# A four-layer graph network on one core: one-hots of the targets compared by VectorE inside the loop, edge steps moved, the tail's products in float32r

## Time and profile before

| | us |
|---|---|
| median of 3 runs (lowest, highest) | 244.22 (243.98, 244.51) |
| the profiled execution | 244.86 |
| its span | 243.1 |
| TensorE busy | 230.7 |
| VectorE busy | 155.0 |
| ScalarE busy | 121.5 |
| GpSimd busy | 5.5 |

### The profile page before, as it was taken

One profiled execution on the slowest core, in us unless ns is written; L12 is line 12 of the kernel. 1 busy time (PEld: TensorE's weight loads), 2 busy tenths in 40 slices (PEclk: granted clock), 3 DMA queues, 4 the chain that ended last, 5 costly groups with the idle time before them and its releaser, 6 DMA issues.

```text
span 243.1 us, 3227 instructions
## 1 busy us (share of the span) xinstructions
PE 230.7 (95%) x1230; PEld 185.8 (76%) x1230; DVE 155.0 (64%) x274; ACT 121.5 (50%) x221; POOL 5.5 (2%) x17
## 2 busy tenths in 40 slices
PE   7999999997999999999999999999999999997980
PEld 4977888664766887888888888888888889996760
DVE  3948765687679655865856848758568455273625
ACT  0617289748639835745635646456356343244000
POOL 0000000001000000000000000000000000000001
PEclk9999999999999999999999999999999999999996
DMA  7999969920580000008041040140000000000001
GB/s 231 288 411 396 391 188 385 380 79 0 167 260 7 0 0 0 3 17 325 3 118 59 0 174 0 10 165 0 0 0 3 0 0 0 3 0 0 3 1 43
DMA packets 12039, 24.97 MB, mean 103 GB/s; under 512 B 988, under 2 KB 1908, under 8 KB 11640
## 3 DMA queue, kind: packets, MB, share of 16 engines
q1 hardware_dynamic: 11232, 24.25, 28.3%
q10 hardware_dynamic: 792, 0.51, 0.8%
HBM read 24.50 MB, written 0.26 MB: 102 GB/s over the span
## 4 chain that ended last, share of the span: by engine, by line
PE 89%; DVE 4%; ACT 2%; issue 2%; POOL 1%; POOLq 0%; DVEq 0%; ACTq 0%
PE bank L675 36%; PE bank L658 12%; PE bank L463 9%; PE bank L472 6%; PE bank L521 4%; PE bank L537 3%; PE bank L685 3%; PE bank L686 3%; PE bank L561 1%; PE bank L482 1%; PE bank L452 1%; ACT WsT L414 1%; PE bank L637 1%; PE bank L549 1%; PE bank L638 1%
## 5 line engine op out<-in xcount | busy, mean ns | idle before, releaser
L675 PE MATMUL bank<-W2hi,Hhi 128*128 128x512 f32 x128 | 49.8, 389 | 0.0
L675 PE MATMUL bank<-W2lo,Hhi 128*128 128x512 f32 x128 | 49.8, 389 | 0.0
L675 PE MATMUL bank<-W2hi,Clo 128*128 128x512 f32 x128 | 49.8, 389 | 0.0
L386 ACT ACTIVATE Mhi<-M 128x512 fp32r<-128x512 f32 x32 | 20.2, 632 | 45.4 <-DVE M L1011 45.4
L1016 DVE TENSOR_TENSOR Mlo<-M,Mhi 128x512 fp32r<-128x512 f32 x32 | 22.1, 689 | 24.4 <-ACT M L387 24.4
L1011 DVE TENSOR_TENSOR M<-bank,b2r 128x512 f32<-128x512 f32 x32 | 22.0, 687 | 12.7 <-PE bank L686 7.6
L675 PEld LDWEIGHTS bank<-W2hi,Hhi 128*128 128x128 f32 x128 | 24.0, 188 | 5.1
L675 PEld LDWEIGHTS bank<-W2lo,Hhi 128*128 128x128 f32 x128 | 24.0, 188 | 5.0
L675 PEld LDWEIGHTS bank<-W2hi,Clo 128*128 128x128 f32 x128 | 24.0, 188 | 5.0
L379 ACT ACTIVATE Hhi<-C 128x512 fp32r<-128x512 f32 x32 | 20.0, 624 | 12.4 <-DVE C L997 12.1
L297 ACT ACTIVATE C<-bank,cols 128x512 f32<-128x512 f32 x32 | 19.9, 685 | 10.5 <-PE bank L521 10.5
(11 more groups left out here) (201 smaller groups left out, 315.5 us busy)
## 6 DMA issues: line engine op xcount, KB each, us to landing
F<-in_L_gnn_W SPq DMA_DIRECT2D x2, 2048.0 KB, 14.6
W1raw<-in_L_gnn_W SPq DMA_DIRECT2D x1, 2048.0 KB, 23.7
ids<-in_src SPq DMA_DIRECT2D x2, 1024.0 KB, 13.1
W<-in_L_gnn_W SPq DMA_DIRECT2D x1, 2048.0 KB, 9.1
Wq<-in_L_gnn_Wq SPq DMA_DIRECT2D x4, 256.0 KB, 3.7
Wk<-in_L_gnn_Wk SPq DMA_DIRECT2D x4, 256.0 KB, 5.4
Wv<-in_L_gnn_Wv SPq DMA_DIRECT2D x1, 1024.0 KB, 9.6
ea<-in_edge_attr SPq DMA_DIRECT2D x1, 1024.0 KB, 11.6
```

Of the source, the lines that this page charges most:

```text
L386: act.activation(Mhi[:, t, :], M[:, t, :], ACT.Mish)
L675: done = mm(ST2[t][:, :], x[:, c, e], w[:, c, :], start=c == 0 and i == 0, stop=c == KC - 1 and i == 2)
```

## The change

1. The eight groups of turned target one-hots, their ScalarE copies and the ring of banks that they used are gone. `DT` is made by VectorE by comparing target ids that are broadcast to all partitions, as `ST` was.
2. Only groups 0 and 1 of `ST` and `DT` are made before the loop (two instructions each). The target ids for them go into the same buffers as the source ids, once these are read. For groups 2 to 7 the ids are loaded a second time and compared inside the loop, two groups ahead; `first_layer(g)` waits for them.
3. Edge steps 0 to 2 stand where the turns stood, step 3 in F1, 4 to 6 in F2.
4. The F2 load no longer waits for the turns; W2's load stands behind the target ids; the rows and weights of the later layers are loaded in the loop's sixth group.
5. The products of W4 and of layer 3 are made of three float32r terms each. The splits of W4, W_self, W_neigh and of their inputs are new instructions on ScalarE and VectorE.
6. The warm-up is six matmuls on a tile that VectorE fills first of all.
7. The softmax's sum over heads is by additions in place of `tensor_reduce`, and the copy `CTs` comes before `uniform`.

```diff
         def first_layer(g, js=range(KC), ks=range(len(terms))):
+                if g >= 2:
+                    pe.wait_ge(S["oh_ready"], 3 * (g - 1))
...
+            def loop_sources(g):
+                dve.wait_ge(S["loop_src_in"], 16)
+                v.tensor_scalar(ST_by_group[:, g], src_ids[:, g // 2, g % 2], iota_col[:, 0:1], None, ALU.is_equal).then_inc(S["oh_ready"], 1)
+            def loop_targets(g):
+                dve.wait_ge(S["loop_dst_in"], 32)
+                for h in range(2):
+                    v.tensor_scalar(DT_by_group[:, g, h], dst_ids[h][:, g // 2, g % 2], iota_col[:, 0:1], None,
+                                    ALU.is_equal).then_inc(S["oh_ready"], 1)
...
                 one_hot(g)
                 z2_out(g, 2)
+                if 1 <= g < G - 2:
+                    loop_sources(g + 2)
+                if g >= G - 2:
+                    weight_low(W4lo, W4, W4hi, (2 * (g - G + 2),), "w4")
                 message_low(g, 2)
                 z2_out(g, 3)
+                if g == 0:
+                    loop_sources(g + 2)
+                elif g < G - 2:
+                    loop_targets(g + 2)
+                if g >= G - 2:
+                    weight_low(W4lo, W4, W4hi, (2 * (g - G + 2) + 1,), "w4")
                 message_low(g, 3)
+                if g == 0:
+                    loop_targets(g + 2)
...
-            source_onehots(0)
+            for h in range(2):
+                first_onehots(ST_by_tile, "row_ids_in", h)
             dve.wait_ge(S["graphT_done"], 1)
...
-            source_onehots(1)
             dve.wait_ge(S["nx_ready"], 2)
             chain(v.tensor_tensor(xw[:, :], y[:, :], r("L0_gnn_b2"), ALU.add))
             xb = r("L0_gnn_be2")
             chain(v.tensor_tensor(xb, xs[:, :], xb, ALU.add))
+            for h in range(2):
+                first_onehots(DT_by_tile, "dst_ids_in", h)
             st = residual((bank[1], bank[2]), xw, S["f2_done"])
...
-            sp.wait_ge(S["pre_done"], C_UNIT)
             sp.wait_ge(S["ct_done"], 1)
             sp.dma_start(F2, w_view(a["L0_gnn_W2"])).then_inc(S["f2_in"], 16)
...
+            for h in range(2):
+                sp.wait_ge(S["st_ready"], h + 1)
+                sp.dma_start(other[f"ids{h}"], by_partition(a["dst"][E // 2 * h:E // 2 * (h + 1)], E // 2)).then_inc(S[f"dst_ids_in{h}"], 16)
             sp.dma_start(W2raw, w_view(a["L1_gnn_W2"])).then_inc(S["w2_in"], 16)
...
             sp.wait_ge(S["nx_ready"], 4)
+            for h in range(2):
+                sp.dma_start(loop_ids[f"dst_ids{h}"], by_partition(a["dst"][E // 2 * h:E // 2 * (h + 1)], E // 2)).then_inc(S["loop_dst_in"], 16)
+                if h == 0:
+                    sp.wait_ge(S["late_done"], 2 * KC)
+                    sp.dma_start(loop_ids["src_ids"], by_partition(a["src"], E)).then_inc(S["loop_src_in"], 16)
...
-            turn_onehots(Dbf, range(1, G))
-            pe.wait_ge(S["ea_lo"], 1)
+            pe.wait_ge(S["cols_ready"], 1)
+            pe.wait_ge(S["wc_lo"], 1)
+            edge_term(range(0, 1))
             turn_features(1)
+            edge_term(range(1, 3))
             transpose_halves(O_BANKS, y, S["nx_ready"], 0, S["nT_done"])
...
-            pe.wait_ge(S["ident_ready"], 1)
-            keep_warm(5, bank[2])
+            pe.wait_ge(S["warm_ready"], 1)
+            keep_warm(6, bank[2])
+            pe.wait_ge(S["ident_ready"], 1)
...
+            pe.wait_ge(S["u_hi"], 2)
+            for b in range(2):
+                columns_by(o_banks, uThi, W4hi, b, (0, 1), 0, None)
+                columns_by(o_banks, uThi, W4lo, b, (0, 1), None, None)
+            pe.wait_ge(S["u_lo"], 1)
+            for b in range(2):
+                columns_by(o_banks, uTlo, W4hi, b, (0, 1), None, None)
...
+            for h in range(2):
+                pe.wait_ge(S["xl_hi"], h + 1)
+                for b in range(2):
+                    columns_by(out_banks, xThi, WsThi, b, (2 * h, 2 * h + 1), None, None)
...
+            weight_low(WsTlo, WsT, WsThi, (1,), "ws")
+            st = bank_statistics((bank[5], bank[6]), S["g3_done"])
+            norms[0] += 1
+            v.bn_aggr(mv[:, :], st).then_inc(S["stat_ready"], 1)
+            weight_low(WsTlo, WsT, WsThi, (2,), "ws")
```

More of the change, by code:

```diff
@@ L77, in gnn_kernel @@
         ones2 = sb("ones2", [2, N], F32R)
+        warm = sb("warm", [P, P], BF16)
         uniform = sb("uniform", [P, N])
@@ L136, in gnn_kernel @@
         W3, W4, WsR, WnR = chunks(last["W3"], 2 * KC), chunks(last["W4"], KC), chunks(last["WsR"], KC), chunks(last["WnR"], KC)
-        WsT, WnT, uT, aggT, nmT = (chunks(last[n], KC) for n in ("WsT", "WnT", "uT", "aggT", "nmT"))
+        WsT, WnT, uT, aggT = (chunks(last[n], KC) for n in ("WsT", "WnT", "uT", "aggT"))
+        W4hi, WsThi, WnThi, xThi, xTlo, nmThi, nmTlo, uThi = (chunks((late if n == "WsThi" else last)[n], KC) for n in (
+            "W4hi", "WsThi", "WnThi", "xThi", "xTlo", "nmThi", "nmTlo", "uThi"))
+        W4lo, WsTlo, WnTlo, uTlo = (chunks(rest[n], KC) for n in ("W4lo", "WsTlo", "WnTlo", "uTlo"))
         G1, G2 = chunks(last["G1"], KC), last["G2"]
@@ L424, in _ @@
             act.activation(r1g, bank[3][:, 0:HID2], ACT.Relu).then_inc(S["g1_ready"], 1)
+            ws_high(2)
             act.wait_ge(S["g2_done"], 1)
             act.activation(p1g, bank[4][:, 0:N], ACT.Copy).then_inc(S["g2_ready"], 1)
+            ws_high(3)
+            act.wait_ge(S["wt_ready"], 2 * KC)
+            for c in range(KC):
+                act.activation(WnThi[:, c, :], WnT[:, c, :], ACT.Copy).then_inc(S["wn_hi"], 1)
+            for h in range(2):
+                act.wait_ge(S["nT_done"], 4 + h + 1)
+                act.activation(half(flat(xThi), h), (bank[1], bank[3])[h][:, 0:D // 2], ACT.Copy).then_inc(S["xl_hi"], 1)
+            act.wait_ge(S["nm_done"], 1)
+            act.activation(flat(nmThi), bank[2][:, :], ACT.Copy).then_inc(S["nm_hi"], 1)
             act.wait_ge(S["y_centred"], 1)
@@ L478, in keep_warm @@
             def keep_warm(n, b):
-                idle = ident[:, :].bitcast(BF16)
                 for _ in range(n):
[L482 to L497, removed]
+                    mm(b[:, :], warm[:, :], warm[:, :].unsqueeze(1).to_broadcast([P, 4, P]), start=True, stop=True)
             def turn_features(q):
@@ L813, in _ @@
             xT_flat = flat(xT[:, :, :])
+            v.memset(warm[:, :], 1.0).then_inc(S["warm_ready"], 1)
             chain(v.memset(stats[:, 2, :], 0.0))
@@ L916, in _ @@
                 dve.wait_ge(S["exp_done"], o + 1)
-                step = v.tensor_reduce(quarter(y, o), attn[:, o].rearrange("p j n -> p n j"), AX.X, ALU.add)
-            chain(step)
+                pairs, four = half(y, 1), quarter(y, o)
+                chain(v.tensor_tensor(pairs, attn[:, o, 0:2].rearrange("p j n -> p (j n)"), attn[:, o, 2:4].rearrange("p j n -> p (j n)"),
+                                      ALU.add))
+                chain(v.tensor_tensor(four, quarter(pairs, 0), quarter(pairs, 1), ALU.add))
             chain(v.tensor_tensor(total[:, :], quarter(y, 0), quarter(y, 1), ALU.add))
@@ L1066, in _ @@
             v.memset(ones, 1.0).then_inc(S["ones_ready"], 1)
+            for h in range(2):
+                dve.wait_ge(S["u_hi"], 2 * (h + 1))
+                dve.wait_ge(S["u_ready"], 2 * (h + 1))
+                v.tensor_tensor(half(flat(uTlo), h), half(flat(uT), h), half(flat(uThi), h).bitcast(F32), ALU.subtract).then_inc(S["u_lo"], 1)
             st = residual((bank[2], bank[4]), xw, S["o_done"])
```

184 lines of the change are left out of this document (115 added, 69 removed).

## The result

The changed kernel takes 247.73 us (247.31 to 248.07, 4 runs), the kernel before 244.10 on the same chip (243.72 to 244.51, 4 runs): ratio 1.0142, interval 1.0123 to 1.0160. That is 3.6 us slower, where 1.0 was forecast, and 0.5 above the upper end of the range. So the two traces are only 2.4 us apart, and 1.2 of the 3.6 can't be read from them.

A forecast was written before the change was run, and what follows sets the result against it. PE, busy 95% of the span, was taken to bound the kernel. Warm-up -0.3, prologue -0.1, group 0 +3.0 and tail -0.6 and -1.0 made +1.0: median 244.22 becomes 245.2, own range 244.6 to 246.2, overall 242.6 to 247.2.

The forecast's parts named there:

- Sum: Whole kernel: warm-up -0.3, prologue -0.1, group 0 +3.0, tail -0.6 and -1.0, giving +1.0 us.
- the third rival: PE's clock falls once in a stall and work behind it runs at half speed: 246.8 us, chance 10%.
- its own two stalls: PE idle 3.15 us before first_layer(2) in the loop, and nearly 3 before the second norm's transposes.
- Group 0: End of loop group 0: PE waits for VectorE's last target compare behind message_low(0,3), cost 3.0 us, bounds 2.8 to 3.2.
- Prologue: Before the loop: PE work saved, but the second norm's residual waits for target-id copies; gain 0.1, bounds -0.8 to +2.4.
- The saving on PE: Up to F2's end: three edge steps fewer after F1's start, so F2 ends at 53.4, not 55.9.
- the landing of the second copy: Second 1 MB target-id copy, before the second norm: issued at 47.2, landed at 54.3 us, bounds 53.4 to 55.7.
- its own signs: Wrong if the residual starts before 53.8, PE doesn't wait in group 1, or the tail's products don't get shorter.
- Start: Warm-up: PE starts 0.65 us sooner and the clock rises sooner; gain 0.3, bounds 0 and 1.5.
- Compares inside groups 1 to 6: Later compares in the loop fit where VectorE waits for ScalarE: value 0, bounds 0 and -1.
- Tail: W4's and layer 3's products in float32r at 0.12 us a matmul: gains 0.6 and 1.1, less 0.1, total 1.6.
- copies land early: Both target-id copies there by 52.7, so the residual starts when F2 is done: 242.8 us, chance 22%.

The follow-up runs named there:

- e3: Changed kernel plus nine idle matmuls on PE before the second layer norm's transposes: ratio 1.0059 to the kernel before, times in two groups, 243.89 to 244.74 and 246.61 to 246.96 us.
- e1: Changed kernel with group 2's source and target compares set earlier in VectorE's order, in gaps waiting for ScalarE: 243.55 us, ratio 0.9963 to the kernel before.
- e4: Kernel before with only the new warm-up (six matmuls on a tile VectorE fills first): 244.14 us beside 244.36, ratio 0.9987.
- e6: Kernel before with only the float32r tail (W4 and layer 3 in three terms, with their splits): 243.21 us, ratio 0.9941.
- e2: Changed kernel plus 12 idle matmuls on PE ahead of its wait for group 2's compares, which stay late: 246.88 us, ratio 1.0106 to the kernel before.
- e7: Changed kernel with group 2's compares early and half 0's source compare before the last two W1lo parts: 240.47 us, ratio 0.9854 to the kernel before.
- e5: Changed kernel with group 2's compares early and nine idle matmuls before the second norm's transposes: 241.97 us, ratio 0.9903 to the kernel before.
- e10: Changed kernel with group 2's compares and half 0's source compare earlier, WsT split behind the norm, four idle matmuls before the second norm's transposes: 239.93 us, ratio 0.9823.

## Why the prediction was wrong

The direction was right, at 55%; the size was not. By its own steps, in the profiled executions:

- *Sum.* The failed step is that the third rival, "the clock falls in a stall", was left out of the sum and given 10%. It happened twice, 1.5 us behind the wait for the norm and 1.6 behind the stall in group 0, 3.1 us against a forecast of 1.0 in all. The earlier trace rows show an idle time of 3.5 us ahead of a fall, and 3.15 and "nearly 3" were the stalls forecast: the prediction took a row with a longer idle time as the only case and did not carry it over to its own two stalls. The traces since show a fall after idle times of 2.25, 2.30, 2.34, 2.65 and 2.82 us, none after 2.81 in another execution and none after 1.14. The row was no measure of how long it takes either: at the end of the twelve traces the fall comes from 1.9 us (after) to 4.8 us (e3) behind PE's last matmul. Rival 3 was priced at 1.6 for one fall (246.8 less 245.2), which is what one measured, but by luck: its working takes a slow start as the model (half of 2.5 us, which is 1.25 and not 1.6), where the falls measured are 3.4 us long. And it allowed for one, not two. The Trainium skill ("TensorE: Matmul & The Clock Gate", section "HAM oscillation — how this bites in real kernels") tells of the same trap: a matmul loop whose waits for data let the clock fall each time round. That the runs agree with; that a stall of 2.3 us can be enough, and that one of 2.8 isn't in every execution, they show beyond it.
- *Group 0.* Forecast 3.0 (2.8 to 3.2), measured 2.8 to 2.9, with DVE's instructions in the order and nearly the lengths named. Right, and e1 confirms it by taking it away.
- *Prologue.* Forecast 0.1 won, measured 1.3 beside the start (2.3 at the transposes, of which 1.0 came from the start). This is read from one pair of traces; no run has the prologue's change alone. The saving on PE was sized well: F2 ends at 52.1, 3.8 sooner than before, and 2.7 without the start, for 2.5 forecast. The mis-sized term is the landing of the second copy: 54.3 forecast, 52.2 measured. 1.2 us of that is the issue (46.0 for 47.2), most of it the earlier start of this execution; the other 0.9 is the copy, 6.2 us from issue to landing for the 7.1 taken. The pair that stood as the model had been queued behind other copies. The first copy took 4.3 us; the 5.2 of the row was too long for it. The Trainium skill's 2 us and bytes over 436 GB/s ("DMA: Bandwidth & Descriptors", "Anatomy of one DMA") makes 4.4, and the first copy agrees; it was weighed and passed over for the row. By its own signs the prediction was wrong here: it named a residual that starts before 53.8, and it started at 52.83; L637's first matmul, expected within 0.7 us of 62.5, came at 60.8.
- *Start.* Forecast 0.3 won; 1.0 in the pair of traces, 0.2 to 0.3 in e4, which is as forecast but can't be told from none. The row of one execution was read as the kernel's; the 4.00 us of Wq's product and its start at 6.53 belong to an execution in which the matmuls became fast late. The upper bound of 1.5 leaves out Wv's copy, on which PE waits in e4's trace. That Wq and Wk went at the lower clock was also misread: 3.77 for 32 is the full-speed figure, as F1's 3.84 is.
- *Compares inside groups 1 to 6.* Forecast 0, measured 0.
- *Tail.* Forecast 1.6, measured 1.4, and 1.2 by itself in medians (e6). 0.120 per matmul was right to a thousandth. The total hides terms that cancel: the split in front of the norm was costed at 0.1 and took 0.33, by pow beside it; layer 3's product gives 1.6 up to its first complete bank where 1.1 was taken for the whole, and the first bank's statistics, no longer hidden inside the product, take 0.4 of that back.

Sum in the traces: -1.0 - 1.3 + 1.5 + 2.9 + 1.6 - 1.4 = +2.3, for 2.4 between the spans. The medians have 3.6. About 0.8 of the rest is the start, won in this pair of traces and by 0.2 to 0.3 only in e4; the last 0.5 stays open. The condition of the "copies land early" rival, both there by 52.7, came true (52.2), and it wasn't faster: half of its 2.5 was won, and that fell to the clock, as the copies' wait and the shorter work ahead of it left PE idle for 2.25 us where it used to have edge steps to do.

## What to carry over

Price a new stall of a busy TensorE at its length, and where it is like the 2.3 and 2.8 us of this kernel, at another 1.5 us for the clock, as the likelier case: here half of the loss came after the waits had ended. When work is moved off an engine's queue, look for the place where this engine now has nothing to do, since an early finish can cost more than it brings. Within one in-order queue try the order before giving up a change: three compares set a few instructions sooner, ahead of subtractions that waited for ScalarE, were worth 4.2 us here.

## What the runs showed of the hardware

- A fall of the granted clock to 0.50 after idle times of 2.25 and 2.82 us, for 3.4 us each time, beginning 0.7 and 1.1 us after work had resumed, at a cost of 1.5 and 1.6 us; the same after 2.34 (e1), 2.65 (e2) and 2.30 (e7), and in another execution none after 2.81 (e3).
- The slow matmuls at the start don't show in the granted clock, which reads 1.00 there in all traces: 0.46 us a matmul of 512 bf16 columns against 0.24 later (e3).
- pow on GpSimd on 128 elements: 0.55 us alone and beside a VectorE `scalar_tensor_tensor` with two inputs in SBUF, 0.88 beside a VectorE subtraction with both operands in SBUF.
- float32r matmuls of 256 columns with a load of weights each run 0.120 us apart, as fast as a float32 half-instruction of 128 columns; the loads of 0.19 don't limit them.
- A 1 MB copy of broadcast rows took 4.3 to 4.7 us, and the one issued 0.6 us behind it 6.2 to 6.6 (after, e1, e2, e3, e5). Issued 3.1 to 3.5 us apart (e7 to e10), the first took 4.9 to 6.3 and the second 4.8 to 6.9.
